# Local convolutions by head: 17 matmul passes with delayed column blocks and shifted copies, in place of 23

## The chip, the core and the metric

The program runs on one core of one Trainium2 chip. Its engines are TensorE (PE, matmuls), VectorE (DVE), ScalarE (ACT), GpSimd (POOL) and SyncE (SP, which only issues transfers). Each runs its own instruction stream and waits on semaphores. The metric is the device time of one execution in microseconds.

## The reference

The input is 16 sequences of 256 tokens with 128 features, all float32. Three blocks follow each other, each with a layer norm and a residual: a mixture of 8 experts (top 2), attention, and the same mixture again. The change is in the attention, in `multiscale_conv`, which acts on the values `v` of 4 heads with 32 channels each:

```python
def multiscale_conv(v, ms_w3, ms_w15, ms_w31, kernel_mix_w, channel_mixer_w):
    b, l, h, d = v.shape
    x = jnp.swapaxes(v.reshape(b, l, h * d), 1, 2)
    outs = [dwconv_causal(x, w) for w in (ms_w3, ms_w15, ms_w31)]
    y = jnp.concatenate(outs, axis=1)
    y = y.reshape(b, h, 3 * d, l).transpose(0, 3, 1, 2)
    y = y @ kernel_mix_w
    y = (y.reshape(b, l, h * d) @ channel_mixer_w).reshape(b, l, h, d)
    return y
```

Three causal convolutions of 3, 15 and 31 taps give 3 x 128 channels. They are laid one behind the other and cut anew into 4 heads of 96 rows. So head 0 reads the kernel of 3 taps alone, head 1 the rest of it and some of the 15 taps, head 2 the rest of the 15 taps and the first 32 channels of the 31 taps, and head 3 the other 96 channels of the 31 taps alone. Each head's 96 rows are mixed to 32 (`kernel_mix_w`), and the 128 results are mixed again (`channel_mixer_w`). Beside it the attention computes a delta rule in chunks of 32 tokens and a small network (gelu, softmax) that weighs convolution, delta rule and `v`; a normalisation and an output projection end it.

## The kernel before

The program is `route`, `experts` ("e1"), `attention`, `experts` ("e2"). In e1 GpSimd folds the convolutions' taps and `kernel_mix_w` into one 128x128 matrix for each lag, `full`, split into a high and a low part for PE (`lag_hi`, `lag_lo`).

**The passes.** A convolution at a lag is a matmul of the lag's matrix with the values shifted by that many tokens. A half `q` (of 8) covers 4 sequences and 128 tokens: one pass is 128x128 by 128x512, and each lag takes three (`vhi` by `lag_hi`, `vlo` by `lag_hi`, `vhi` by `lag_lo`). `scales(q, at, count)` (L1066) issues passes number `at` and onward. The far lags 15 to 30 fill only half of the output columns, so a pass takes two of them, the second in the other column half, to be delayed by one token when it is copied out: 8 orders in bank 0. The near lags 0 to 14 take 15 orders in bank 1. That is 23 orders, 69 passes a half.

**Behind them.** ACT copies the sums from PSUM: `keep_far` (three copies, two of which place the delayed half) and `keep_near` (one copy). `channels(q)` (L1214) multiplies both by `channel_mixer_w`, 8 instructions, and `keep_scales` copies the result.

**The stages.** The sequences are worked in 4 groups of 4. Stage g, from -1 to 3, runs the delta rule of group g while it projects and convolves group a = g+1 (`stage`, L1316). It has 16 slots: each of the 8 steps is a `read` (L1168), a slot, an `update` (L1188), a slot. A slot holds large passes: the keys and queries of group a (`keys`), then `scales(2g+1)` by the numbers in `SCALES_AT` (L1412; `SCALES_ALONE` in the last stage), then its values. After the slots comes a tail: for the halves of group g the hidden layer (`hide`), `logits`, `turn_means`, `turn_mixture` and `output`, with pieces of `scales(2a)` between them (`filler`), and then `channels(2a)`, `turn(g+2)` and the solving of the next group's chunks.

**What sets the order.** It is written out by hand for each engine, and each executes strictly in that order. In ACT's stage `route_power` (an exponential for the routing of the group before, L1952) comes before `silu_queries(a, 1)` (L1857). The far and near sums use the same two banks as the projections, so the first pass into a bank waits until its last content has been copied: `silued` for the queries, `zkept` for the sums. In the tail ACT's order is an exponential (`power`, L1925), gelu (L1920), `keep_far` (L1895 to L1897), square (L1929), exponential, root (L1933), `keep_mixture` (L1938), square, root, `keep_near` (L1902).

## Time and profile before

| | us |
|---|---|
| median of 3 runs | 1018.54 |
| lowest, highest | 1016.92, 1025.63 |
| profiled execution, its own time | 1015.78 |
| its span in the profile | 1014.0 |
| mean granted clock of PE, share of full speed | 0.938 |

The profiled execution is the shortest of the four numbers, so durations read from it belong to 1015.78 and not to the median. The attention takes roughly the stretch from 320 to 730 us of the span; what lies before and after it is routing and experts. Busy times of PE are modelled at the end of an instruction: passes that are shown with 0.40 us start 0.24 us apart.

### The profile page before, as it was taken

The numbers are of one execution on the slowest core, as the hardware profiler recorded it, in microseconds if no ns is written. First come the engines' busy times: TensorE is split into PE (matmuls) and PEld (weight loads), VectorE is DVE, ScalarE is ACT, GpSimd is POOL, SyncE is SP. The second block draws the span as 40 slices with busy tenths as digits, with TensorE's granted clock in tenths as the row PEclk, the third lists the DMA queues.
The fourth block names the chain that finished last, engine by engine and source line by source line (L and its number), as shares of the span: only waits on it lengthen the run. The fifth ranks groups of instructions, "written<-read, shape, count | busy, mean of one in ns | idle before, by whom it ended". The sixth has DMA issues, their size and how long they took to land. (4 is left out here: it accounts for less than half of the span.)

```text
span 1014.0 us, 27996 instructions
## 1 busy us (share of the span) xinstructions
PE 878.8 (87%) x11972; PEld 768.5 (76%) x11972; DVE 569.9 (56%) x1663; ACT 338.9 (33%) x648; POOL 448.7 (44%) x550
## 2 busy tenths in 40 slices
PE   7739998999858889997999899979873999999980
PEld 5629998999846667776777777867762899999980
DVE  6806556555366953575566635562462455555545
ACT  2214443444214121342325331521241444444420
POOL 2757897254533002850058036814603234444442
PEclk9859999999959979999999999998997999999995
DMA  8833543442140000000100000001100433433326
GB/s 287 325 112 112 161 140 98 134 127 78 38 109 22 1 6 22 2 1 3 35 4 1 8 29 14 2 7 33 47 7 28 136 107 115 129 120 128 121 80 171
DMA packets 66550, 78.56 MB, mean 77 GB/s; under 512 B 8752, under 2 KB 52704, under 8 KB 65402
## 3 DMA queue, kind: packets, MB, share of 16 engines
q1 hardware_dynamic: 57466, 60.03, 19.3%
q0 software_dynamic: 8960, 16.74, 5.1%
q8 instruction: 94, 1.54, 0.6%
q14 instruction: 30, 0.25, 0.1%
HBM read 47.92 MB, written 30.52 MB: 77 GB/s over the span
## 5 line engine op out<-in xcount | busy, mean ns | idle before, releaser
L763 DVE TENSOR_TENSOR e_hid<-e_sg,e_pu 128x320 f32<-128x320 f32 x256 | 124.6, 487 | 165.8 <-ACT e_sg L699 162.2
L256 POOL DMA_INDIRECT queue<-xn,slot x128 | 127.5, 996 | 182.8 <-PE a_pc L1188 59.8
L267 POOL DMA_INDIRECT token<-e_rows,e_token x120 | 121.2, 1010 | 153.9 <-DVE e_rows L729 111.0
L699 ACT ACTIVATE e_sg<-e_pg 128x320 f32<-128x320 f32 x256 | 112.2, 438 | 207.9 <-PE e_pg L654 207.7
L652 PE MATMUL e_pg<-e_xlo,e_whi 128*128 128x320 f32 x256 | 96.1, 375 | 6.4 <-DVE e_xlo L718 3.3
L625 PE MATMUL e_po<-expert,e_hid 128*128 128x128 f32 x640 | 84.2, 275 | 0.0
L1082 PE MATMUL a_pz<-a_vhi,lag_hi 128*128 128x512 f32 x184 | 79.3, 431 | 2.5 <-DVE a_vlo L1480 2.5
L625 PEld LDWEIGHTS e_po<-expert,e_hid 128*128 128x128 f32 x640 | 80.3, 191 | 0.1
L654 PE MATMUL e_pu<-e_xhi,e_whi 128*128 128x320 f32 x256 | 79.5, 311 | 0.0
L653 PE MATMUL e_pu<-e_xhi,e_wlo 128*128 128x320 f32 x256 | 79.5, 311 | 0.0
L652 PE MATMUL e_pu<-e_xlo,e_whi 128*128 128x320 f32 x256 | 79.4, 310 | 0.0
L653 PE MATMUL e_pg<-e_xhi,e_wlo 128*128 128x320 f32 x256 | 79.3, 310 | 0.0
L654 PE MATMUL e_pg<-e_xhi,e_whi 128*128 128x320 f32 x256 | 79.2, 309 | 0.0
L1082 PE MATMUL a_pz<-a_vlo,lag_hi 128*128 128x512 f32 x184 | 78.1, 425 | 0.0
L1082 PE MATMUL a_pz<-a_vhi,lag_lo 128*128 128x512 f32 x184 | 77.0, 418 | 0.0
L625 PE MATMUL e_po<-e_expert,e_hid 128*128 128x128 f32 x560 | 73.7, 275 | 0.0
L625 PEld LDWEIGHTS e_po<-e_expert,e_hid 128*128 128x128 f32 x560 | 70.5, 191 | 0.0
L262 POOL DMA_INDIRECT expert<-rows,slot x24 | 22.7, 947 | 98.8 <-DVEq L1451 75.6
L840 POOL TENSOR_TENSOR a_prod<-a_inv,a_nmat 128x31 f32<-128x31 f32 (+15 forms) x93 | 48.3, 519 | 38.0 <-DVE a_nmat L1532 31.0
L842 POOL TENSOR_TENSOR a_inv<-a_inv,a_prod 128x31 f32<-128x31 f32 (+15 forms) x93 | 58.1, 625 | 7.3
L652 PEld LDWEIGHTS e_pg<-e_xlo,e_whi 128*128 128x128 f32 x256 | 49.0, 192 | 8.4 <-issue 6.7
L653 PEld LDWEIGHTS e_pg<-e_xhi,e_wlo 128*128 128x128 f32 x256 | 49.2, 192 | 0.0
(303 smaller groups left out, 1902.8 us busy)
## 6 DMA issues: line engine op xcount, KB each, us to landing
e_xs<-queue SPq DMA_DIRECT2D x32, 322.5 KB, 3.5
expert<-wexp_in SPq DMA_DIRECT2D x14, 512.0 KB, 5.2
e_expert<-wexp_in SPq DMA_DIRECT2D x14, 512.0 KB, 5.4
queue<-r_zero SPq DMA_DIRECT2D x4, 1290.0 KB, 10.2
token<-r_zero SPq DMA_DIRECT2D x4, 1024.0 KB
expert<-wexp_in SPq DMA_DIRECT2D x14, 256.0 KB, 2.9
e_expert<-wexp_in SPq DMA_DIRECT2D x14, 256.0 KB, 2.7
xn<-token SPq DMA_DIRECT2D x7, 512.0 KB, 7.6
```

The costliest lines, as they stand in the source:

```text
L256: pool.indirect_dma_start(io.queue[c], bass.IndirectOffsetOnAxis(ap=k.slot[:, j, c:c + 1], axis=0), k.xn[:, j, :], None, bounds_check=SLOT ...
L262: pool.indirect_dma_start(dst, None, io.rows, bass.IndirectOffsetOnAxis(ap=slot, axis=0)).then_inc(got, 16)
L267: pool.indirect_dma_start(io.token[c], bass.IndirectOffsetOnAxis(ap=token, axis=0), src, None, bounds_check=NTOK - 1, oob_is_err=False).th ...
L625: mm = pe.matmul(po[:, s // 4, (s % 4) * P:(s % 4) * P + P], hid[par][:, f, s * P:s * P + P], w[par][:, 2, f * P:f * P + P], start=(f == 0 ...
L652: pe.matmul(out, whi[par][:, i, fs], xlo[par][:, cols], start=True, stop=False)
L653: pe.matmul(out, wlo[par][:, i, fs], xhi[par][:, cols], start=False, stop=False)
L654: pe.matmul(out, whi[par][:, i, fs], xhi[par][:, cols], start=False, stop=True).then_inc(gued, 1)
L699: act.activation(sg[n % 2][:], pg[n % 2][:, 0:HALF], ACT.Silu).then_inc(silued, 1)
L763: dve.tensor_tensor(hid[q % 2][:, f, c * HALF:c * HALF + HALF], sg[n % 2][:], pu[n % 2][:, 0:HALF], ALU.mult).then_inc(hidden, 1)
L840: link(eng.tensor_tensor(part, bc(inv[:, j:j + 1, 0:j + 1], shape), bc(factor, shape), ALU.mult))
L842: link(eng.tensor_tensor(rest, rest, part, ALU.add))
L1082: mm = pe.matmul(pz[:, bank, :].rearrange("p (s l) -> p s l", s=SEQS), w[:, j, :], x[:, :, start:start + P], start=first, stop=last)
```

## The change

The orders are packed by head. Order 0 ("apart") holds four lags of column blocks that need nothing more: head 0's three lags and head 3's lag 15. Each block is copied out with its own delay (0, 1, 2 and 15 tokens). Head 0 then needs no further pass, so its 32 columns in the 15 near orders carry head 3's lags 16 to 30, to be delayed by 16 tokens. Head 2's part of the 31 taps covers only 32 channels, and its lags 15 to 30 go into a single order ("stacked", order 11): SP copies those 32 channels four times below each other, shifted by 0, 1, 2 and 3 tokens (`shi`, `slo`), and the four column blocks are delayed by 0, 4, 8 and 12. That makes 17 orders, 51 passes a half. The column blocks that belong to the same head are summed in `channels`, whose weights (`channel_rows`) repeat the head's rows: three matmuls for a chunk in place of two. The blocks are placed by ACT, 32 partitions at a time: 7 copies for apart, 7 for stacked, 3 for near (`keep_part`). The counts in slots and fillers are smaller, and `load_expert` for e2 moves behind the copies of three groups.

```diff
@@ -47,7 +47,9 @@
 PAD = TAPS - 1
 LAGS = 31
 NEAR = 15
-FAR = (LAGS - NEAR) // 2
+ROWS = P // DH
+SPILL = 16
+PASSES = 2 + NEAR
 GRP = 8
 YB = NT
 SEQS = GRP * P // SEQ
...
@@ -179,38 +182,42 @@
-    def fold_far(self, pool, k):
...
+    def fold_apart(self, pool, k):
+
         w31 = lambda lag: self.ms31[:, LAGS - 1 - lag:LAGS - lag]
+        head = lambda h: slice(h * DH, h * DH + DH)
+        for lag in range(3):
+            pool.tensor_scalar(self.full[:, 0, head(lag)], self.base[:, 0, head(0)], self.ms3[:, 2 - lag:3 - lag], None,
+                               ALU.mult)
+        pool.tensor_scalar(self.full[:, 0, head(3)], self.base[:, 2, head(3)], w31(NEAR), None, ALU.mult)
+        for i in range(ROWS):
+            pool.tensor_scalar(self.full[:, 1, head(i)], self.mixs[:], self.ms31s[:, i:i + 1], None, ALU.mult)
+        for n in range(NEAR):
+            pool.tensor_scalar(self.full[:, 2 + n, head(3)], self.base[:, 2, head(3)], w31(n + SPILL), None, ALU.mult)
...
@@ -854,7 +861,9 @@
     UNITS, TURNS, TERMS = 6, 8, 3
     QUARTERS, QN = 4, NCH // 4
     KEYS, VALUES = 4 * TERMS * TAPS + 2 * TERMS, 2 * TERMS * TAPS
-    FARS, SCALES = TERMS * FAR, TERMS * (FAR + NEAR)
+    SCALES = TERMS * PASSES
+    STACKED_AT = 11
+    Z_APART, Z_STACKED, Z_NEAR = 0, 1, 2
     strip = lambda i: slice(i * CHUNK, i * CHUNK + CHUNK)
     with ExitStack() as ctx:
         m = Memory(nc, ctx)
...
@@ -945,10 +955,21 @@
+            for a in range(NGRP):
+                if a == NGRP - 1:
+                    sp.wait_ge(loaded[1], 16 * (NGRP - 1))
+                    sp.wait_ge(combined, NGRP)
+                    load_expert(sp, io, k.w, 0, loaded[1])
+                for half in range(HALVES):
+                    behind(sp, zdone, 6 * a + 3 * half - 1)
+                    for done, part, stack in ((vhigh, vhi, shi), (vlow, vlo, slo)):
+                        sp.wait_ge(done, 2 * a + 2)
+                        for r in range(ROWS):
+                            at = LAGS - 1 - NEAR - r + half * P
+                            sp.dma_start(stack[r * DH:r * DH + DH, :, :].bitcast(F32),
+                                         part[0:DH, :, at:at + P].bitcast(F32)).then_inc(shifted, 16)
+            sp.wait_ge(loaded[1], 16 * NGRP)
+            sp.wait_ge(shifted, 16 * 2 * ROWS * HALVES * NGRP)
 
         @block.gpsimd
         def _(pool):
...
@@ -1066,21 +1087,30 @@
             def scales(q, at, count):
                 a, half = divmod(q, 2)
                 for i in range(at, min(at + count, SCALES)):
-                    j, term = divmod(i, TERMS)
-                    lag = NEAR + 2 * j if j < FAR else j - FAR
-                    bank = 0 if j < FAR else 1
-                    first, last = i in (0, FARS), i in (FARS - 1, SCALES - 1)
-                    if first and half and a + 1 < NGRP:
+                    order, term = divmod(i, TERMS)
+                    kind = {0: Z_APART, STACKED_AT: Z_STACKED}.get(order, Z_NEAR)
+                    lag = order - 1 - (order > STACKED_AT) if kind == Z_NEAR else 0
+                    bank = 1 if kind == Z_NEAR else 0
+                    first = i == 0 or i == TERMS or i == TERMS * STACKED_AT
+                    last = i == TERMS - 1 or i == TERMS * STACKED_AT + TERMS - 1 or i == SCALES - 1
+                    if first and kind == Z_STACKED:
+                        pe.wait_ge(zkept, 3 * q + 1)
+                        pe.wait_ge(shifted, 16 * 2 * ROWS * (q + 1))
+                    elif first and half and a + 1 < NGRP:
                         pe.wait_ge(silued, UNITS * (a + 1) + 3 + bank)
                     elif first and half:
-                        pe.wait_ge(zkept, 4 * a + 1 + bank)
+                        pe.wait_ge(zkept, 6 * a + 2 + bank)
                     elif first:
                         pe.wait_ge(silued, UNITS * a + 5 + bank)
                         pe.wait_ge(vlow, 2 * a + 2)
-                    x, w = ((vhi, k.lag_hi), (vlo, k.lag_hi), (vhi, k.lag_lo))[term]
-                    start = LAGS - 1 - lag + half * P
-                    mm = pe.matmul(pz[:, bank, :].rearrange("p (s l) -> p s l", s=SEQS), w[:, j, :],
-                                   x[:, :, start:start + P], start=first, stop=last)
+                    if kind == Z_STACKED:
+                        x, w = ((shi, k.lag_hi), (slo, k.lag_hi), (shi, k.lag_lo))[term]
+                        start = 0
+                    else:
+                        x, w = ((vhi, k.lag_hi), (vlo, k.lag_hi), (vhi, k.lag_lo))[term]
+                        start = LAGS - 1 - lag + half * P
+                    mm = pe.matmul(pz[:, bank, :].rearrange("p (s l) -> p s l", s=SEQS), w[:, kind + lag, :],
+                                   x[:, :, start:start + P], start=term == 0 and (kind < Z_NEAR or lag == 0), stop=last)
                     if last:
                         mm.then_inc(zdone, 1)
                 return min(at + count, SCALES)
...
@@ -1213,16 +1243,16 @@
...
                 for i in range(HCH):
-                    pe.matmul(pp[:, 1, i * P:i * P + P], chunks(znear[:], i), k.chan[:], start=True, stop=False)
-                    mm = pe.matmul(pp[:, 1, i * P:i * P + P], chunks(zfar[:], half * HCH + i), k.chan_far[:],
-                                   start=False, stop=True)
+                    for n, part in enumerate(z):
+                        mm = pe.matmul(pp[:, 1, i * P:i * P + P], chunks(part[:], half * HCH + i), k.chan[:, n, :],
+                                       start=(n == 0), stop=(n == 2))
                 mm.then_inc(chaned, 1)
 
             def turn_means(q):
...
@@ -1375,20 +1405,20 @@
...
-                part = filler(9)
+                part = filler(6)
                 idle(g, 9)
                 if here:
                     hide(2 * g + 1, 0)
                     hide(2 * g + 1, 1)
-                part = filler(12)
+                part = filler(9)
                 idle(g, 4)
                 if here:
                     logits(2 * g + 1)
-                part = filler(12)
+                part = filler(9)
                 idle(g, 24)
                 if here:
                     turn_mixture(2 * g)
-                part = filler(9)
+                part = filler(6)
                 idle(g, 3)
                 if here:
                     output(2 * g)
...
@@ -1409,11 +1439,11 @@
                     solve_keys(a, 0)
 
             KEYS_AT = (12, 8, 12, 8, 14)
-            SCALES_AT = (0, 0, 0, 0, 0, 8, 7, 7, 7, 7, 8, 8, 8, 9)
-            SCALES_ALONE = (5, 4, 6, 4, 6, 6, 6, 6, 6, 6, 6, 6, 2)
+            SCALES_AT = (0, 0, 0, 0, 0, 6, 6, 5, 5, 5, 6, 6, 6, 6)
...
@@ -1885,22 +1915,35 @@
                 act.activation(u[:, half * HCH:half * HCH + HCH, :, :].rearrange("p n s d -> p (n s d)"), pp[:, 2, :],
                                ACT.Copy).then_inc(ukept, 1)
 
-            def keep_far(q):
-                half = q % 2
-                act.wait_ge(zdone, 2 * q + 1)
+            def keep_part(q, kind, first, end, delay):
+                head, at = slice(first * DH, end * DH), q % 2 * HCH
+                raw = pz[head, kind // 2, :].rearrange("p (s n c) -> p n s c", s=SEQS, n=HCH)
+                last = act.activation(z[kind][head, at:at + HCH, :, delay:], raw[:, :, :, 0:CHUNK - delay], ACT.Copy)
+                if delay:
+                    over = HCH - q % 2
+                    last = act.activation(z[kind][head, at + 1:at + over + 1, :, 0:delay],
+                                          raw[:, 0:over, :, CHUNK - delay:], ACT.Copy)
+                return last
+
+            def keep_apart(q):
+                act.wait_ge(zdone, 3 * q + 1)
                 behind(act, chaned, q)
-                far = D // 2
-                z = pz[:, 0, :].rearrange("p (s n c) -> p n s c", s=SEQS, n=HCH)
-                at = half * HCH
-                act.activation(zfar[0:far, at:at + HCH, :, 1:], z[0:far, :, :, 0:CHUNK - 1], ACT.Copy)
-                act.activation(zfar[0:far, at + 1:at + HCH + 1, :, 0:1], z[0:far, :, :, CHUNK - 1:], ACT.Copy)
-                act.activation(zfar[far:D, at:at + HCH, :, :], z[far:D], ACT.Copy).then_inc(zkept, 1)
+                for h, delay in enumerate((0, 1, 2, NEAR)):
+                    last = keep_part(q, Z_APART, h, h + 1, delay)
+                last.then_inc(zkept, 1)
+
+            def keep_stacked(q):
+                act.wait_ge(zdone, 3 * q + 2)
+                behind(act, chaned, q)
+                for i in range(ROWS):
+                    last = keep_part(q, Z_STACKED, i, i + 1, ROWS * i)
+                last.then_inc(zkept, 1)
 
             def keep_near(q):
-                act.wait_ge(zdone, 2 * q + 2)
+                act.wait_ge(zdone, 3 * q + 3)
                 behind(act, chaned, q)
-                act.activation(znear[:], pz[:, 1, :].rearrange("p (s n c) -> p n s c", s=SEQS, n=HCH),
-                               ACT.Copy).then_inc(zkept, 1)
+                keep_part(q, Z_NEAR, ROWS - 1, ROWS, SPILL)
+                keep_part(q, Z_NEAR, 0, ROWS - 1, 0).then_inc(zkept, 1)
 
             def keep_scales(q):
                 act.wait_ge(chaned, q + 1)
...
@@ -1979,10 +2022,12 @@
                     root_keys(a)
                 if later:
                     root_rows(g + 2)
+                if here:
+                    keep_apart(2 * g + 1)
                 if ahead and here:
                     measure(a)
                 if here:
-                    keep_far(2 * g + 1)
+                    keep_stacked(2 * g + 1)
                     keep_values(g, 0)
                     keep_values(g, 1)
                     keep_near(2 * g + 1)
...
@@ -2000,11 +2045,11 @@
                     gelu(2 * g, 1)
                     keep_means(2 * g + 1)
                     power(2 * g)
+                if ahead:
+                    keep_apart(2 * a)
                 if here:
                     gelu(2 * g + 1, 0)
                     gelu(2 * g + 1, 1)
-                if ahead:
-                    keep_far(2 * a)
                 if here:
                     square(2 * g)
                     power(2 * g + 1)
...
@@ -2013,6 +2058,7 @@
                     square(2 * g + 1)
                     root_mix(2 * g + 1)
                 if ahead:
+                    keep_stacked(2 * a)
                     keep_near(2 * a)
                     keep_scales(2 * a)
                 if later:
...
```

**ScalarE, in the tail of stage 1**, between the exponential of the second half and the square of the first (`a_lg` are the logits, `a_hdn` the hidden layer, `a_pz` the sums in PSUM). Before:

```order
L1925 ACTIVATE a_lg<-a_lg 128x48 [waits a_lowered]
L1920 ACT_TABLE_LOAD [waits a_scored,a_gated]
L1920 ACTIVATE a_hdn<-a_pp,b 128x512 [waits a_hidden]
L1920 ACTIVATE a_hdn<-a_pp,b 128x512 [waits a_scored,a_gated,a_hidden]
L1895 ACTIVATE a_zfar<-a_pz 64x16x31 [waits a_chaned,a_zdone]
L1896 ACTIVATE a_zfar<-a_pz 64x16
L1897 ACTIVATE a_zfar<-a_pz 64x512
L1929 ACTIVATE a_direct<-a_delta 128x512 [waits a_mixed]
```

and changed:

```order
L1968 ACTIVATE a_lg<-a_lg 128x48 [waits a_lowered]
L1921 ACTIVATE a_z<-a_pz 32x512 [waits a_chaned,a_zdone]
L1921 ACTIVATE a_z<-a_pz 32x16x31
L1924 ACTIVATE a_z<-a_pz 32x16
L1921 ACTIVATE a_z<-a_pz 32x16x30
L1924 ACTIVATE a_z<-a_pz 32x16x2
L1921 ACTIVATE a_z<-a_pz 32x16x17
L1924 ACTIVATE a_z<-a_pz 32x16x15
L1963 ACT_TABLE_LOAD [waits a_scored,a_gated]
L1963 ACTIVATE a_hdn<-a_pp,b 128x512 [waits a_hidden]
L1963 ACTIVATE a_hdn<-a_pp,b 128x512 [waits a_scored,a_gated,a_hidden]
L1972 ACTIVATE a_direct<-a_delta 128x512 [waits a_mixed]
```

The copies of bank 0 stand ahead of gelu now, and there are seven in place of three.

**ScalarE, at the end of the same tail**, from the last square. Before:

```order
L1929 ACTIVATE a_direct<-a_delta 128x512 [waits a_mixed]
L1933 ACTIVATE a_ors<-a_oss,eps 128x16 [waits a_summed]
L1902 ACTIVATE a_znear<-a_pz 128x512 [waits a_chaned,a_zdone]
L1908 ACTIVATE a_ms<-a_pp 128x512 [waits a_mixed,a_chaned]
L1938 ACTIVATE a_oT<-a_pc 128x4x4x32 [waits a_done,a_oturned]
```

and changed:

```order
L1972 ACTIVATE a_direct<-a_delta 128x512 [waits a_mixed]
L1976 ACTIVATE a_ors<-a_oss,eps 128x16 [waits a_summed]
L1921 ACTIVATE a_z<-a_pz 32x512 [waits a_chaned,a_zdone]
L1921 ACTIVATE a_z<-a_pz 32x16x28
L1924 ACTIVATE a_z<-a_pz 32x16x4
L1921 ACTIVATE a_z<-a_pz 32x16x24
L1924 ACTIVATE a_z<-a_pz 32x16x8
L1921 ACTIVATE a_z<-a_pz 32x16x20
L1924 ACTIVATE a_z<-a_pz 32x16x12
L1921 ACTIVATE a_z<-a_pz 32x16x16 [waits a_chaned,a_zdone]
L1924 ACTIVATE a_z<-a_pz 32x16x16
L1921 ACTIVATE a_z<-a_pz 96x512
```

Behind the root, where one copy stood, there are ten: seven of the stacked order and three of the near orders.

**TensorE, in slot 5 of stage 1**, from the delta rule's output matmuls of the update to the next read (`a_sq` are the squares of keys and queries). Before:

```order
L1194 MATMUL a_po<-a_u,a_loc 32x32 x16
L1082 MATMUL a_pz<-a_vhi,lag_hi 128x512 [waits a_silued]
L1082 MATMUL a_pz<-a_vlo,lag_hi 128x512
L1082 MATMUL a_pz<-a_vhi,lag_lo 128x512
L1082 MATMUL a_pz<-a_vhi,lag_hi 128x512
L1093 MATMUL a_pp<-const,a_sq 64x4 [waits a_mskept,a_squared]
L1093 MATMUL a_pp<-const,a_sq 64x4 x7
L1082 MATMUL a_pz<-a_vlo,lag_hi 128x512
L1082 MATMUL a_pz<-a_vhi,lag_lo 128x512
L1082 MATMUL a_pz<-a_vhi,lag_hi 128x512
L1082 MATMUL a_pz<-a_vlo,lag_hi 128x512
L1168 MATMUL a_pc<-a_state,a_wT 32x32 [waits a_stated]
```

and changed:

```order
L1224 MATMUL a_po<-a_u,a_loc 32x32 x16
L1112 MATMUL a_pz<-a_vhi,lag_hi 128x512 [waits a_silued]
L1112 MATMUL a_pz<-a_vlo,lag_hi 128x512
L1112 MATMUL a_pz<-a_vhi,lag_lo 128x512
L1123 MATMUL a_pp<-const,a_sq 64x4 [waits a_mskept,a_squared]
L1123 MATMUL a_pp<-const,a_sq 64x4 x7
L1112 MATMUL a_pz<-a_vhi,lag_hi 128x512 [waits a_silued]
L1112 MATMUL a_pz<-a_vlo,lag_hi 128x512
L1112 MATMUL a_pz<-a_vhi,lag_lo 128x512
L1198 MATMUL a_pc<-a_state,a_wT 32x32 [waits a_stated]
```

The slot has six passes in place of eight, and its fourth, the first of the near orders, carries a wait for `silued` that stood at the 25th pass of the half before.

## Rows read from the trace of the kernel before

**Rows 1.** The page's first part: busy time, share of the span, instructions.
```profile
PE 878.8 (87%) x11972; PEld 768.5 (76%) x11972; DVE 569.9 (56%) x1663; ACT 338.9 (33%) x648; POOL 448.7 (44%) x550
```
**Rows 2.** Windows: stretch, length, busy time by engine, clock, DMA share, GB/s.
```profile
core 0: us, PE busy (x) PEld busy (x) DVE busy (x) ACT busy (x) POOL busy (x), PEclk, DMA share, GB/s
362.00:428.00 66.00, 64.18 (x1662) 48.28 (x1654) 31.72 (x85) 15.11 (x25) 27.26 (x44) 0.98 0.04 11
536.00:567.00 31.00, 29.00 (x155) 23.36 (x154) 23.51 (x41) 15.58 (x23) 16.99 (x29) 1.00 0.00 1
680.00:729.00 49.00, 42.87 (x1312) 32.65 (x1299) 17.89 (x87) 7.00 (x13) 25.30 (x26) 0.91 0.12 37
467.00:471.00 4.00, 4.00 (x31) 2.67 (x33) 2.38 (x17) 1.53 (x2) 0.00 (x0) 0.57 0.02 4
```
**Rows 3.** Timeline of PE, tail of stage 0: start, duration, what, idle before it.
```profile
452.94 0.39 PE L1082 MATMUL a_pz<-a_vlo,lag_hi 128*128 128x512 f32 x1
...
456.01 0.40 PE L1082 MATMUL a_pz<-a_vhi,lag_lo 128*128 128x512 f32 x1
```
**Rows 4.** Timeline of PE, end of stage -1.
```profile
356.91 0.32 PE L1139 MATMUL a_pp<-a_vh,a_low 32*32 32x32 f32 x6 [5.25 <-DVE a_low L1540]
```
**Rows 5.** Timeline of PE, tail of stage 1.
```profile
551.23 1.85 PE L1260 MATMUL a_pp<-w,a_hdn 128*128 128x12 f32 x16
...
557.30 0.66 PE L1270 MATMUL a_pp<-const,a_delta 128*128 128x128 f32 x4 [1.30 <-DVE a_delta L1631]
...
565.24 0.49 PE L1223 MATMUL a_pp<-chan,a_znear 128*128 128x128 f32 x2 [0.69 <-ACT a_znear L1902]
...
567.13 1.04 PE L1021 MATMUL a_pz<-const,xn 128*128 128x128 f32 x8
```
**Rows 6.** Timeline of ACT and PE, slot 5, and of ACT, tail, of stage 1.
```profile
496.37 0.21 ACT L1952 ACTIVATE a_ratio<-a_gap 128x8 f32<-128x8 f32 x1 [4.39 <-DVE a_gap L1647]
...
497.89 0.60 ACT L1857 ACTIVATE a_kq<-a_pz 128x512 f32<-128x512 f32 x1
497.90 0.45 PE L1168 MATMUL a_pc<-a_state,a_wT 32*32 32x32 f32 x32
...
546.46 0.24 ACT L1925 ACTIVATE a_lg<-a_lg 128x48 f32<-128x48 f32 x1
...
549.29 0.58 ACT L1895 ACTIVATE a_zfar<-a_pz 64x496 f32<-64x496 f32 x1
549.77 0.18 ACT L1896 ACTIVATE a_zfar<-a_pz 64x16 f32<-64x16 f32 x1
549.96 0.59 ACT L1897 ACTIVATE a_zfar<-a_pz 64x512 f32<-64x512 f32 x1
552.27 0.63 ACT L1929 ACTIVATE a_direct<-a_delta 128x512 f32<-128x512 f32 x1 [1.71 <-DVE a_delta L1621]
...
562.69 0.31 ACT L1933 ACTIVATE a_ors<-a_oss,eps 128x16 f32<-128x16 f32 x1 [0.75 <-DVE a_oss L1625]
564.59 0.60 ACT L1902 ACTIVATE a_znear<-a_pz 128x512 f32<-128x512 f32 x1 [1.59 <-PE a_pz L1082]
```
**Rows 7.** Timeline of DVE, slots 9 to 13 of stage 1.
```profile
512.66 0.62 DVE L1518 TENSOR_TENSOR a_low<-a_pp,a_bvk 128x256 f32<-128x256 f32 x1 [2.17 <-PE a_pp L1121]
...
518.67 4.78 DVE L1466 TENSOR_SCALAR xn<-x,a_mv,a_rstd 128x128 f32<-128x128 f32 x8
523.37 0.28 DVE L1554 TENSOR_TENSOR a_u<-a_u,a_pc 128x128 f32<-128x128 f32 x1
```
**Rows 8.** Timeline of PE, start of stage 1.
```profile
466.13 0.25 PE L1154 MATMUL a_po<-a_nmat,a_kn 32*32 32x32 f32 x5 [1.95 <-issue]
...
467.68 0.63 PE L1027 MATMUL a_pz<-a_xhi,tap_lo 128*128 128x512 f32 x1
...
470.24 0.63 PE L1027 MATMUL a_pz<-a_xhi,tap_lo 128*128 128x512 f32 x1
```
**Rows 9.** The page's sixth part: transfers by line, KB each, us to landing.
```profile
xn<-token SPq DMA_DIRECT2D x7, 512.0 KB, 7.6
```

71 lines of the change are left out of this document (38 added, 33 removed).

## Prediction, made before the changed kernel was run

> **What bounds the kernel now.** I read the page's totals first, then the windows of the attention part, then the timeline of TensorE (PE) and ScalarE (ACT) where the changed work stands. The totals make PE the candidate: busy 87% of the span [rows 1]. The windows say where that is true. In the slots of stage 0 PE is busy 64.18 of 66.00 us at a granted clock of 0.98 [rows 2]; in the tail of stage 1 it is busy 29.00 of 31.00 us [rows 2], but its large passes there are filler, placed between steps of a chain that runs through ACT and VectorE (DVE). So a removed pass is worth its time only where PE would otherwise have been the last to arrive.
>
> A pass costs its pitch, not its busy time of 0.40 us, whose end is modelled. Fourteen passes start from 452.94 to 456.01 [rows 3], 13 steps: **0.236 us**.
>
> **What is removed and added on PE.** Each of the 8 halves loses 6 lags of 3 terms, 18 passes, 4.25 us; over 8 halves 34.0 us. `channels` grows from 8 to 12 instructions: 8 take 565.24 to 567.13, 1.89 us [rows 5], so 4 more are **+0.9 us** per half, 7.2 us in all. Were PE alone the bound, the balance would be -26.8 us. The following goes through the places one by one.
>
> **Stage -1.** PE waits 5.25 us for DVE before `solve_values` [rows 4]; the 18 passes removed ahead of it lengthen that wait. Saving 0. The added 0.9 us of `channels` stands ahead of the same wait and is covered too.
>
> **Slots of stages 0 to 3** (`scales(2g+1)`: 18 passes less, 4.25, less 0.9 for `channels`: at most -3.35 us each).
> - Stage 0: PE-bound throughout [rows 2], but DVE's eight normalising instructions take 4.78 us in a row ahead of a subtraction (the same in stage 1, at 518.67 [rows 7]), which I let take 0.4 back: **-3.0**.
> - Stage 1: a new wait. The first near pass comes fourth now, not 25th, so it stands in slot 5; its bank is released by `silu_queries(a,1)`, which ACT starts at 497.89 and ends at 498.49, behind `route_power` (an exponential at 496.37, then a table load) [rows 6]. Before, that slot ended with the read at 497.90 [rows 6]. Now three near passes follow 498.49: the read comes at about 499.3, +1.4, with the slot's own two saved passes in it. Queued behind the waiting pass is the whole recurrence. Slots 6 to the middle of 9 save 6 passes, -1.4. From there DVE is bound: it works from 512.66 to 523.45 almost without a gap, ends with the normalising and only then does the subtraction for which `update(1, 6)` waits [rows 7]; of the passes saved there I count 0.5. Slot 13 saves 3, -0.7; `channels` +0.9. Sum -0.3, rounded for the small delays of the longer ACT copies to **0.0**.
> - Stage 2: the same wait in slot 5 (+1.4) but no normalising; slots 6 to 13 save 16 passes, -3.8, `channels` +0.9: **-1.5**.
> - Stage 3: four passes per slot are left where there were mostly six; the window has PE busy 42.87 of 49.00 us [rows 2], so nearly all of the 3.35 counts: **-3.2**.
> Sum of the slots **-7.7**. `keep_stacked(2g+1)` stands ahead of `keep_values` on ACT and delays it by some 2 us; PE needs that copy's bank a slot later, over 3 us, so it costs nothing; without that distance it would cost up to 2 us per stage.
>
> **Tails of stages 0 to 2**, by stage 1's. The chain goes: ACT's exponential at 546.46, DVE's mixture, ACT's square at 552.27, and by way of sums, a root and a rescaling to `turn_mixture` at 557.30, before which PE already waited 1.30 us [rows 5, 6]. Nothing in it is a filler pass: removing 9 passes ahead of `turn_mixture` saves **0**, and its wait grows. `keep_apart(2a)` now stands right behind the exponential and delays gelu by its 2.5 us: gelu ended at 549.28, when `keep_far` started [rows 6], and ends at 551.8. PE, 0.7 us earlier than before and with 9 fillers rather than 12 behind `hide`, would be at `logits(2g+1)` at 549.8 instead of 551.23 [rows 5] and waits 2 us; logits end 0.6 us later than before, and ACT is free for the square at 552.27 [rows 6]. DVE takes those logits only after a sum behind the square, so the chain stands: 0.
>
> **The end of the tail** is where I expect the loss. Before, ACT did one copy of 0.60 us behind the second root (562.69 to 563.00), and it waited 1.59 us for PE's last pass; `channels` started at 565.24 [rows 5, 6]. Now `keep_stacked` (7 copies) and `keep_near` (3) both stand behind that root. No row shows copies of 32 partitions; the nearest are of 64: 496 elements occupy ACT 0.48 us (549.29 to 549.77), 16 elements 0.19 (to 549.96) [rows 6]. Between them, by elements (512, 448+64, 384+128, 320+192), `keep_stacked` takes 0.49 + 0.67 + 0.67 + 0.67 = 2.5 us, and `keep_near` 0.33 + 0.33 + 0.5 = 1.2. Bounds: 0.49 for every copy gives 3.4 and 1.5; a cost by elements alone (2.0 and 1.0) the other end. ACT, not PE, is last: 563.00 + 3.7 = 566.7, **+1.5** (bounds +0.8 to +2.7), and `channels` itself +0.9: +2.4 per tail. Behind it stand `turn(g+2)` and `solve_values`; PE goes straight on there [rows 5], so it is not given back. Three tails: **+7.2**.
>
> **The clock.** PE now idles some 4 us ahead of `channels` instead of 0.69 [rows 5]. After a wait of 1.95 us at 466.13 the passes from 467.68 to 470.24 stand 0.427 us apart, not 0.236, and the granted clock of that stretch is 0.57, the 1.2 GHz level for most of it [rows 2, 8]: seven passes, 1.3 us lost. I take one such stretch for each tail, 3.9, less one that stage 0 has already in this place (the one of rows 8): **+2.6**. Bounds: 0 (the idle shifts, it adds none) and twice that.
>
> **What costs nothing.** The 16 copies of 32 channels per group, issued by SP: no row has a copy within the on-chip memory; the nearest are 512 KB in 7.6 us [rows 9], each of these is 64 KB. The passes that read them are 33 passes behind the start of their half, over 8 us of passes alone and 15 us with what stands between them, and the buffers are free since the last half. If they came late, the stacked passes would wait with everything behind them (rival 3). SP also holds back the load of the next experts' weights behind the copies of groups 0 to 2; it is used only after the attention. GpSimd's folding of weights lies in the first experts part, beside PE work, and gets slightly shorter.
>
> **The sum.** -7.7 + 7.2 + 2.6 = **+2.1 us**. The profiled execution took 1015.78 (span 1014.0), so the changed one 1017.9. The median of the runs shown, 1018.54, lies 2.76 above the profiled one: **1020.7 us**. Its own range, from the bounds (copies -2.1/+3.6, clock -2.6/+2.6, slot waits -3/+3) and the scatter of the runs: 1012 to 1029.
>
> **Rivals.**
> 1. PE-bound everywhere. For it: 87% busy, windows of 93 to 97%. Against: PE's waits of 5.25 and 1.30 us stand just where passes are removed [rows 4, 5]. It would give -26.8: 991.7. Chance 0.07. The Trainium skill's page "Perfetto Trace Analysis", section "Identifying the Most-Contended Engine", says to optimise the engine with the highest occupancy first, and that TensorE's headroom is not judged by matmul busy time; its first half points to this rival, its second is why busy time is weak evidence here.
> 2. Slots give all, tails lose nothing. Copies of 32 partitions are as cheap as the lower bound and hidden, and the slot-5 wait is not there because `silu_queries` comes early when PE runs ahead. 4 x -3.35 = -13.4: 1005.1. For it: stage 0's window [rows 2]. Against: slot 5's rows [rows 6]. Chance 0.15.
> 3. Slower: the tail's end. From the point where the ten copies take over 4.5 us (or the stacked copies land late), PE idles over 5 us ahead of `channels`, and the whole of `turn`, `solve` and the first `keys` runs at the lower clock. Copies at the upper bound add 1.2 per tail; low-clock stretches three times those of rows 8 add 2.6 more: 3 x 3.8 = 11.4 over the forecast: 1032. For it: ACT's late place is certain from the order of the program. Against: ACT's interpolated prices. Chance 0.18.
>
> The forecast has 0.60. Within 1% of 1018.54 (1008.4 to 1028.7; about what a measurement of this kernel tells from no change) lies most of the forecast: 0.56 there, 0.02 on either side. Rival 2 lies below 1008.4, as does 1: faster 0.24; slower 0.20. The range that holds 8 in 10 leaves out rival 1 and the upper half of rival 3: **1003 to 1031**.
>
> **What would show it.** PE in stage 1's slot 5 idles 1.5 to 2 us before a near pass, released by ACT's `a_kq` copy (right), or not (rival 2). Each of the first three tails shows PE idle 3 to 5 us ahead of `channels`, released by ACT's last `a_z` copy; ACT's seven stacked copies sum to 2.2 to 2.8 us. `turn_mixture(2g)` stands as far behind the exponential as before (10.8 us). The granted clock in the slices behind the tails falls below 0.9. Wrong it would be if the idle time ahead of `channels` stays under 2 us, if the slots of stages 0 and 3 do not get 3 us shorter, or if a pass waits for SP's copies.

## The result and the profile after

| | before | changed |
|---|---|---|
| median of 20 runs, us | 1018.64 | 1023.42 |
| lowest, highest | 1012.49, 1025.63 | 1018.29, 1031.44 |
| profiled execution, its span | 1015.78, 1014.0 | 1022.46, 1020.4 |
| mean granted clock | 0.938 | 0.923 |

The ratio is 1.0057 (95% interval 1.0039 to 1.0076): 5 to 6 us slower, within 1%. The forecast was +2.1 us, 1020.7 for the median.

The first part of the page of the changed kernel, for [rows 1]:

```profile
PE 863.1 (85%) x11892; PEld 757.5 (74%) x11892; DVE 565.2 (55%) x1665; ACT 373.0 (37%) x752; POOL 444.3 (44%) x557
```

PE has 15.7 us less to do and the span is 6.4 us longer: PE's busy time was not what the end hung on. ACT has 34.1 us more.

Where time goes and comes back is read by subtracting the starts of the same instruction in both traces:

| first instruction of | before | changed | later by |
|---|---|---|---|
| `solve_values`, group 0 | 356.91 | 353.46 | -3.45 |
| `update`, step 0, stage 0 | 366.43 | 364.27 | -2.16 |
| `channels`, slot 15, stage 0 | 425.16 | 418.39 | -6.77 |
| `solve_values` behind tail 0 | 460.39 | 458.80 | -1.59 |
| `update`, step 0, stage 1 | 470.80 | 466.29 | -4.51 |
| `update`, step 2 (ahead of slot 5), stage 1 | 493.90 | 489.56 | -4.34 |
| `update`, step 3, stage 1 | 501.67 | 501.26 | -0.41 |
| `channels`, slot 15, stage 1 | 533.31 | 530.39 | -2.92 |
| `turn_mixture(2)` | 557.30 | 555.42 | -1.88 |
| `channels` at the end of tail 1 | 565.24 | 564.76 | -0.48 |
| `solve_values` behind tail 1 | 568.53 | 570.57 | +2.04 |
| `update`, step 0, stage 2 | 576.25 | 578.33 | +2.08 |
| `channels`, slot 15, stage 2 | 639.28 | 641.28 | +2.00 |
| `solve_values` behind tail 2 | 673.63 | 681.82 | +8.19 |
| `update`, step 0, stage 3 | 679.78 | 687.42 | +7.64 |
| `channels`, slot 15, stage 3 | 726.13 | 728.44 | +2.31 |
| `turn_mixture(7)` | 753.56 | 756.96 | +3.40 |
| span | 1014.0 | 1020.4 | +6.4 |

The attention of the kernel before starts at 296 us and reaches `turn_mixture(7)` at 754, so its stretch is wider than the 320 to 730 given above. Of the +6.4 us of the span, three parts can be told apart: -3.4 ahead of its first gate pass (303.06, not 306.50), +6.8 from there to `turn_mixture(7)`, and +3.0 behind that.

**Ahead of the attention.** The program differs there only in what GpSimd folds. The last folding instruction, which makes `lag_lo`, has 2176 columns for 2944 and takes 4.89 us for 6.80. In both kernels one VectorE instruction of the first experts part starts while it runs and ends only when it has ended. Before, that was one that PE needed:

```profile
164.62 6.80 POOL L220 TENSOR_TENSOR lag_lo<-full,lag_hi 128x2944 fp32r<-128x2944 f32 x1
166.64 5.33 DVE L710 TENSOR_TENSOR e_wlo<-expert,e_whi 128x512 fp32r<-128x512 f32 x1
172.51 0.39 PE L652 MATMUL e_pg<-e_xlo,e_whi 128*128 128x320 f32 x1 [2.91 <-DVE e_hid L763]
```

and changed, where PE has no wait behind it:

```profile
160.92 4.89 POOL L227 TENSOR_TENSOR lag_lo<-full,lag_hi 128x2176 fp32r<-128x2176 f32 x1
162.88 2.95 DVE L746 TENSOR_SCALAR e_token<-e_xs 128x5 uint32<-128x5 f32 x1
```

The same VectorE instruction (`e_wlo`) takes 0.68 us when nothing holds it. The first gate pass starts at 303.1 to 304.6 in the changed kernel and in E2, E3, E4, E9, E10 and E12, which fold as it does, and at 309.2 in E1, which folds as before. In E11 it starts at 306.4 although it folds as the changed kernel: there VectorE's `e_token` is held for 4.81 us and PE waits 1.81. So the gain belongs to the change in most executions; no run separates it, and why VectorE is held isn't shown.

**Inside the attention.** Slots gain (from the first `update`, 4.6 us in stage 0 and 5.3 in stage 3), each tail loses 5 to 6, and stages 1 and 2 gain next to nothing in their slots, for the most part because of one wait in slot 5. E9, the same kernel once more, loses 10.2 us by the same cut in its profiled execution, which took 1027.72: its tails agree (+15.4 for +16.3 us) and its slots gain less (3.9 for 8.4). Single terms of the slots are thus good to some microseconds only.

**Behind it.** The 3.0 us are lost before the second experts part, at a granted clock of 0.69 in the window from 763 to 773 us, where the same stretch before (760 to 770) has 1.00. E2, E4 and E9 lose 2.5 to 3.5 us there as well, E3, E10, E11 and E12 0 to 1.0, so it is not a fixed price of the change.

Slot 5 of stage 1, PE and then ACT, timelines of the changed kernel (start, duration, what, idle before it):

```profile
490.25 0.51 PE L1112 MATMUL a_pz<-a_vhi,lag_hi 128*128 128x512 f32 x1
490.59 0.40 PE L1112 MATMUL a_pz<-a_vlo,lag_hi 128*128 128x512 f32 x1
490.83 0.40 PE L1112 MATMUL a_pz<-a_vhi,lag_lo 128*128 128x512 f32 x1
491.15 1.09 PE L1123 MATMUL a_pp<-const,a_sq 128*64 128x4 f32 x16
494.21 0.79 PE L1112 MATMUL a_pz<-a_vhi,lag_hi 128*128 128x512 f32 x1 [1.96 <-ACT a_kq L1887]
494.80 0.63 PE L1112 MATMUL a_pz<-a_vlo,lag_hi 128*128 128x512 f32 x1
495.23 0.63 PE L1112 MATMUL a_pz<-a_vhi,lag_lo 128*128 128x512 f32 x1
495.78 0.65 PE L1198 MATMUL a_pc<-a_state,a_wT 32*32 32x32 f32 x32
```
```profile
492.04 0.21 ACT L1995 ACTIVATE a_ratio<-a_gap 128x8 f32<-128x8 f32 x1 [4.37 <-DVE a_gap L1677]
492.26 1.28 ACT L1887 ACT_TABLE_LOAD   x1
493.56 0.60 ACT L1887 ACTIVATE a_kq<-a_pz 128x512 f32<-128x512 f32 x1
```

The first near pass waits 1.96 us for a copy that itself stood behind an exponential [rows 6]. What the wait leaves behind costs time as well: the passes behind it start 0.43 us apart instead of 0.24, and the window says why. Windows of the changed kernel: the slots of stage 0, tail 1, the slots of stage 3, the stretch behind that wait, and `channels` in tail 1:

```profile
358.00:422.00 64.00, 62.63 (x1718) 47.03 (x1714) 31.05 (x85) 19.39 (x38) 26.37 (x43) 0.95 0.05 12
534.00:570.00 36.00, 29.99 (x154) 24.39 (x153) 23.76 (x41) 20.34 (x38) 17.78 (x30) 0.91 0.19 52
682.00:731.00 49.00, 41.64 (x1563) 32.28 (x1553) 19.93 (x92) 12.49 (x28) 24.50 (x25) 0.95 0.12 37
494.00:500.00 6.00, 5.79 (x134) 4.24 (x134) 1.04 (x5) 4.95 (x12) 0.00 (x0) 0.50 0.01 3
565.00:569.00 4.00, 4.00 (x23) 4.00 (x23) 0.35 (x1) 0.00 (x0) 0.00 (x0) 0.57 0.02 4
```

The tail of stage 1 had a granted clock of 1.00 [rows 2] and has 0.91; the six microseconds behind slot 5's wait run at 0.50, the 1.2 GHz level.

The middle of tail 1, PE, of the changed kernel, from the logits to `turn_mixture(2)`:

```profile
549.78 1.95 PE L1290 MATMUL a_pp<-w,a_hdn 128*128 128x12 f32 x16 [1.55 <-ACT a_hdn L1963]
...
553.32 0.63 PE L1112 MATMUL a_pz<-a_vlo,lag_hi 128*128 128x512 f32 x1
553.74 0.63 PE L1112 MATMUL a_pz<-a_vhi,lag_lo 128*128 128x512 f32 x1
...
555.42 0.66 PE L1300 MATMUL a_pp<-const,a_delta 128*128 128x128 f32 x4
```

PE waits for gelu, ahead of which the seven apart copies now stand, and the nine fillers behind the logits run 0.43 us apart. So PE reaches `turn_mixture` with no wait in tails 0 and 1, and with 1.67 us of it in tail 2, where these fillers run 0.24 apart.

The end of tail 1, ACT and then PE, of the changed kernel; the first row is the root behind which one copy stood [rows 6]:

```profile
560.81 0.31 ACT L1976 ACTIVATE a_ors<-a_oss,eps 128x16 f32<-128x16 f32 x1 [0.75 <-DVE a_oss L1655]
561.02 1.12 ACT L1921 ACTIVATE a_z<-a_pz 32x512 f32<-32x512 f32 x2
562.05 0.20 ACT L1924 ACTIVATE a_z<-a_pz 32x64 f32<-32x64 f32 x1
562.26 0.48 ACT L1921 ACTIVATE a_z<-a_pz 32x384 f32<-32x384 f32 x1
...
563.47 0.36 ACT L1921 ACTIVATE a_z<-a_pz 32x256 f32<-32x256 f32 x1
563.73 0.36 ACT L1924 ACTIVATE a_z<-a_pz 32x256 f32<-32x256 f32 x1
564.11 0.59 ACT L1921 ACTIVATE a_z<-a_pz 96x512 f32<-96x512 f32 x1
```
```profile
564.76 4.57 PE L1254 MATMUL a_pp<-chan,a_z 128*128 128x128 f32 x24 [4.23 <-ACT a_z L1921]
569.17 1.04 PE L1042 MATMUL a_pz<-const,xn 128*128 128x128 f32 x8
```

The seven stacked copies take 561.02 to 563.47, 2.45 us; the near ones until 564.70, 1.23. PE idles 4.23 us where it idled 0.69, and then runs `channels` in 4.41 us (564.76 to 569.17) where 8 instructions took 1.89 [rows 5]. In stage -1 the same 24 matmuls take 2.78 us to the next start, behind 1.34 us of idle time, so 1.6 us of it is clock. In tails 0 and 2 PE idles 3.26 and 4.23 us and `channels` takes 4.15 and 5.28.

### The profile page after: what moved, and what is told of

Its sections match the earlier page's. It is cut to its first block and busy times, and to the rows that moved or that the text cites. A ratio compares the mean times of both kernels' runs of the same rounds, so it can differ in the third digit from the quotient of the medians.

```text
span 1020.4 us, 28035 instructions
## 1 busy us (share of the span) xinstructions
PE 863.1 (85%) x11892; PEld 757.5 (74%) x11892; DVE 565.2 (55%) x1665; ACT 373.0 (37%) x752; POOL 444.3 (44%) x557
## 5 line engine op out<-in xcount | busy, mean ns | idle before, releaser
L847 POOL TENSOR_TENSOR a_prod<-a_inv,a_nmat 128x31 f32<-128x31 f32 (+15 forms) x93 | 50.3, 540 | 41.1 <-DVE a_nmat L1562 34.1
L1112 PE MATMUL a_pz<-a_vhi,lag_hi 128*128 128x512 f32 x128 | 59.9, 468 | 6.5 <-ACT a_kq L1887 3.9
L849 POOL TENSOR_TENSOR a_inv<-a_inv,a_prod 128x31 f32<-128x31 f32 (+15 forms) x93 | 55.8, 599 | 7.3
L1112 PE MATMUL a_pz<-a_vlo,lag_hi 128*128 128x512 f32 x128 | 55.0, 430 | 0.0
L1112 PE MATMUL a_pz<-a_vhi,lag_lo 128*128 128x512 f32 x128 | 54.6, 426 | 0.0
L1921 ACT ACTIVATE a_z<-a_pz 32x512 f32<-32x512 f32 (+3 forms) x80 | 40.9, 512 | 28.7 <-PE a_pz L1112 28.0
```

Source lines behind the costliest of these rows:

```text
L847: link(eng.tensor_tensor(part, bc(inv[:, j:j + 1, 0:j + 1], shape), bc(factor, shape), ALU.mult))
L849: link(eng.tensor_tensor(rest, rest, part, ALU.add))
L1112: mm = pe.matmul(pz[:, bank, :].rearrange("p (s l) -> p s l", s=SEQS), w[:, kind + lag, :], x[:, :, start:start + P], start=term == 0 and ...
L1921: last = act.activation(z[kind][head, at:at + HCH, :, delay:], raw[:, :, :, 0:CHUNK - delay], ACT.Copy)
```

## The experiments

Twelve more runs were made, in three rounds. Ratios are to the kernel before, run in the same round: its median is 1017.31 us beside E1 to E4, 1057.56 beside E5 to E8, and 1019.90 beside E9 to E12, so only ratios compare between rounds. The changed kernel stands at 1.0057 and, run again as E9, at 1.0043: 1.005. It did not run in the rounds of E1 to E8, and where a run is compared with it there, this 1.005 is carried over, with an interval of about 0.002 of its own.

**E1, lags dropped: what the missing passes are worth.** The kernel before, less six far orders, with the counts of the changed kernel in slots and fillers:

```diff
-    FARS, SCALES = TERMS * FAR, TERMS * (FAR + NEAR)
+    FARS, SCALES = TERMS * 2, TERMS * (2 + NEAR)
```

> The kernel before, with the last six of its eight far orders left out (18 of 69 passes per half, so the output lacks those lags) and the slot and filler counts of the changed kernel. All else is as before: four copies on ScalarE, two matmuls per chunk in channels, no transfers by SP. It prices the removal of passes alone. My theory: only the slots pay (13 us over four stages, less than 4 x 4.25 because VectorE takes some back), and in each of three tails channels starts 1.5 us earlier, when the root is done: about -17 us, 1002. Rival (TensorE is the bound everywhere): 8 x 4.25 = -34, 985. If it lies near 1018, even the slots pay nothing.

Measured 1005.6, ratio 0.9895 (0.9863 to 0.9927): -10.7 us, of 34 that the passes take. The rival of a PE-bound kernel is out, and my own -17 was too high. New idle time shows why; PE's waits in tails 0 and 1:

```profile
448.31 0.66 PE L1270 MATMUL a_pp<-const,a_delta 128*128 128x128 f32 x4 [3.08 <-DVE a_delta L1631]
454.54 0.49 PE L1223 MATMUL a_pp<-chan,a_znear 128*128 128x128 f32 x2 [1.16 <-ACT a_znear L1902]
...
551.14 0.66 PE L1270 MATMUL a_pp<-const,a_delta 128*128 128x128 f32 x4 [3.12 <-DVE a_delta L1631]
```

`turn_mixture` waited 1.30 [rows 5] and waits 3.1: the fillers ahead of it were free in the kernel before.

**E2, one copy of each kind: what ACT's pieces cost.**

```diff
-                for i in range(ROWS):
-                    last = keep_part(q, Z_STACKED, i, i + 1, ROWS * i)
+                last = keep_part(q, Z_STACKED, 0, ROWS, 0)
```
(and the same for the other two kinds)

> The changed kernel with one copy of 128x512 for each of the three kinds of sums instead of 7, 7 and 3 (the delays are left out, so the convolution is wrong). Passes, waits, transfers and matmuls stay. My theory: behind the root of each tail stand 1.2 us of copies instead of 3.7, so channels starts 2.5 us earlier in three tails, and the low-clock stretch behind the idle time shrinks by 0.5 to 1 each: -9 to -10 us from 1023.4, about 1014. Rival (the loss sits in the third matmul of channels, in slot 5 or in SP's transfers): within 3 us of 1023.

Measured 1008.29, ratio 0.9924 (0.9894 to 0.9955): -1.3% of the changed kernel's time, some -13 us, more than the 9 to 10 expected. ACT at the end of tail 1:

```profile
553.43 0.31 ACT L1973 ACTIVATE a_ors<-a_oss,eps 128x16 f32<-128x16 f32 x1 [0.75 <-DVE a_oss L1655]
553.64 1.06 ACT L1921 ACTIVATE a_z<-a_pz 128x512 f32<-128x512 f32 x2
```

Two copies of 128 partitions take 1.06 us for the ten pieces' 3.68. PE then idles 1.64 us ahead of `channels` in tails 0 and 1 and 0.69 in tail 2, and `channels` takes 2.78 us in all three. So E2 takes away the copies' length and the lower clock behind it together: the pieces with what they cause are enough to turn the sign, for without them the kernel lies below the one before.

**E3, three passes in slot 5.**

```diff
-            SCALES_AT = (0, 0, 0, 0, 0, 6, 6, 5, 5, 5, 6, 6, 6, 6)
+            SCALES_AT = (0, 0, 0, 0, 0, 3, 6, 6, 6, 6, 6, 6, 6, 6)
```

> The changed kernel with 3 passes in slot 5 (the apart order alone) and 6 in every later slot (0,0,0,0,0,3,6,6,6,6,6,6,6,6), so that the first near pass stands in slot 6, behind a read. My theory: the idle time of 1.96 us before it in stages 1 and 2 goes, and with it the stretch at the lower clock behind it (six passes 0.43 apart, a gram of 1.93 for 1.10): 2 to 2.5 us per stage net of what VectorE keeps, -4 to -5, about 1019. Rival (it only moves into slot 6, or VectorE's chain takes it all): within 1.5 us of 1023.4.

Measured 1019.48, ratio 1.0029 (1.0002 to 1.0056), some 2 us below the changed kernel and not clear of noise: the intervals overlap. The wait got shorter and did not go; the first near pass in slot 6 of stages 1 and 2:

```profile
494.68 0.50 PE L1112 MATMUL a_pz<-a_vhi,lag_hi 128*128 128x512 f32 x1 [1.07 <-ACT a_kq L1887]
...
604.85 0.76 PE L1112 MATMUL a_pz<-a_vhi,lag_hi 128*128 128x512 f32 x1 [1.02 <-ACT a_kq L1887]
```

Here, moving work away from a late event only halved the wait and moved it; the event has to come earlier.

**E4, the stacked copies ahead of the second square.**

```diff
                     keep_mixture(2 * g)
+                if ahead:
+                    keep_stacked(2 * a)
+                if here:
                     square(2 * g + 1)
                     root_mix(2 * g + 1)
                 if ahead:
-                    keep_stacked(2 * a)
                     keep_near(2 * a)
```

> The changed kernel with keep_stacked(2a) on ScalarE right behind keep_mixture(2g), ahead of the second square, where the trace has 2.71 us of idle time, instead of behind the last root. My theory: the seven copies (2.45 us) fit there, only keep_near (1.23) stays behind the root, and channels starts 2.2 us earlier in each of three tails, with a smaller stretch at the lower clock: -7 to -10, about 1015. Rival (the copies do not fit and delay square and root by as much): within 2 us of 1023.4; then the tail's end is bound by ScalarE's whole load.

Measured 1013.51, ratio 0.9965 (0.994 to 0.999): -9 us from the changed kernel. ACT in tail 1:

```profile
555.78 0.60 ACT L1981 ACTIVATE a_oT<-a_pp 128x512 f32<-128x512 f32 x1 [1.76 <-PE a_pp L1300]
556.28 1.12 ACT L1921 ACTIVATE a_z<-a_pz 32x512 f32<-32x512 f32 x2
...
558.51 0.31 ACT L1924 ACTIVATE a_z<-a_pz 32x192 f32<-32x192 f32 x1
559.09 0.63 ACT L1972 ACTIVATE a_direct<-a_delta 128x512 f32<-128x512 f32 x1 [0.27 <-DVE a_delta L1651]
```

They end before the square could start: it still waits 0.27 us for DVE. PE's wait ahead of `channels` falls from 4.23 to 1.91 us, and `channels` takes 2.78 us.

**E5, the exponential behind the queries.**

```diff
-                if past:
-                    route_power(r)
                 if ahead:
                     silu_queries(a, 1)
+                if past:
+                    route_power(r)
+                if ahead:
                     root_keys(a)
```

> The changed kernel with ScalarE's route_power moved behind silu_queries(a,1), so that the bank of the near passes is freed before slot 5 and not behind an exponential that waits for VectorE. My theory: the idle time of 1.96 us in slot 5 of stages 1 and 2 and the low-clock stretch behind it go: -4 to -6 from 1023.4, about 1018.5. In the trace no near pass of stages 1 and 2 waits for a_kq. Rival (VectorE's chain in slots 9 to 13 binds the stage anyway): -2 or less.

Ratio 1.0021 (0.9998 to 1.0045), 0.3% below the changed kernel, about -3 us and so less than the 4 to 6 expected; the intervals touch. No near pass of stages 1 and 2 waits for `a_kq` any more. Around slot 5 the changed kernel lost 3.9 us in stage 1 and 2.7 in stage 2 (+2.23 at 601.41, +4.88 at 611.83), so 6.6 in all. In E5's trace the stretch between the updates of steps 2 and 3 takes 7.06 and 9.03 us in stages 1 and 2, in E6 of the same round, which keeps the wait, 11.49 and 11.24. The wait is thus removed and a part of what that saves is taken back behind; which link takes it was not separated.

**E6, dummy matmuls in the idle time: is it the clock?**

```diff
                 part = filler(SCALES)
+                if ahead and here:
+                    keep_clock(pe, k, pp[:, 1, :], 30)
```

> The changed kernel with 30 dummy matmuls (bf16, 128x256, about 3.4 us, into the PSUM bank that channels writes next) behind the last filler pass in the tails of stages 0 to 2, where TensorE idles 3.3 to 4.2 us. They remove idle time and no work. My theory: channels starts when it did (ScalarE's copies decide), but runs at the high level, 2.9 us and not 4.3 to 4.6, and what follows too: -1.5 per tail, -4 to -5 from 1023.4, about 1019. Rival (the slow channels is not due to the idle time ahead of it): 1023 or, with dummies in the way, later.

Ratio 1.0001 (0.9975 to 1.0027): -0.5% from the changed kernel, 5 us, by work that computes nothing; the interval just touches that of E9. PE at the end of tail 0, and the window with `channels` in it:

```profile
470.50 3.45 PE L479 MATMUL a_pp<-const 128*128 128x256 bf16 x30
473.82 2.94 PE L1254 MATMUL a_pp<-chan,a_z 128*128 128x128 f32 x24
476.61 1.04 PE L1042 MATMUL a_pz<-const,xn 128*128 128x128 f32 x8
```
```profile
474.00:478.00 4.00, 4.00 (x36) 3.84 (x36) 0.52 (x2) 1.19 (x3) 0.00 (x0) 1.00 0.02 4
```

`channels` takes 2.79 us to the next start, not 4.15, at a clock of 1.00. From the start of `channels` to `solve_values` the three tails take 4.2, 4.2 and 3.3 us, in the changed kernel 5.6, 5.8 and 6.0: 5.6 us less, with the same instructions in between, which agrees with the ratio.

**E7, E4's and E5's moves together.**

> The changed kernel with both moves on ScalarE: keep_stacked(2a) ahead of the second square, and route_power behind silu_queries(a,1). The places are apart, so the gains should add: -9 and -5 from 1023.4, about 1009, which is 9 us faster than the kernel before. Rival (one wait covers the other): not below 1013.

Ratio 0.9893 (0.9857 to 0.9929): -1.6%, against -0.9% and -0.3% alone. They add, within the intervals.

**E8, dummies on top (14).**

> As the run before, with 14 dummy matmuls (1.6 us) in the idle time of about 1.9 us that is left ahead of channels in three tails. My theory: channels of stage 0's tail, and what follows in the others, keeps the high level: -1 to -3 from the run before, about 1007. Rival: the idle time left is too short to matter, no difference beyond 1 us.

Ratio 0.988 (0.984 to 0.9919). Not to be told from E7, although the dummies did what they were for: `channels` takes 2.78 us in all three tails, in E7 4.08, 2.78 and 4.41. A gain of 2.9 us lies within the noise of two times six executions, so E8 neither confirms nor refutes E6.

**E9, the changed kernel again.**

> The changed kernel itself once more, unaltered, as the reference for the three runs beside it. Ratio to the kernel before as measured first: 1.0057 (1.004 to 1.008). Rival: if it lies at 1.000 or at 1.012 here, chips differ by as much as the effects, and differences between the runs of different chips below 0.6% mean nothing.

1025.32, ratio 1.0043 (1.0024 to 1.0062).

**E10, no transfers.**

```diff
-                            sp.dma_start(stack[r * DH:r * DH + DH, :, :].bitcast(F32),
-                                         part[0:DH, :, at:at + P].bitcast(F32)).then_inc(shifted, 16)
+                            pass
```
(with the waits on `shifted` gone and the four copies set to zero once)

> The changed kernel without SP's 64 transfers of 32 channels (the four shifted copies are zeros throughout, so the stacked order adds nothing). Passes, ScalarE's copies and channels stay. My theory: the copies land long before the passes that read them: no difference from the run of the changed kernel beside it beyond 2 us. Rival (they hold back TensorE or other transfers): 4 us or more faster.

1033.58, ratio 1.012 (1.0085 to 1.0155): *slower* than E9 by 8 us, which neither theory has. Its six runs lie from 1025.14 to 1039.23; the profiled one is the fastest (span 1023.3 against E9's 1025.6), and in its trace `channels` of tail 0 starts at 452.95, E9's at 453.04. So the trace shows no cost of the transfers and none of leaving them out. The five slower executions have a mean granted clock of 0.905 to 0.914, the profiled one 0.922 and E9's twelve 0.912 to 0.925: they were slower at a lower clock. What lowered it no profile shows, and it stays open. That the transfers are hidden rests on the changed kernel's trace: no row of a stacked pass waits for them, and a transfer lands in 2.1 us:

```profile
a_shi<-a_vhi SPq DMA_DIRECT2D x32, 64.0 KB, 2.1
```

**E11, two matmuls in `channels`.**

```diff
-                    for n, part in enumerate(z):
+                    for n, part in ((0, z[0]), (2, z[2])):
```

> The changed kernel with two matmuls per chunk in channels, the stacked sums left out of the product (they are still computed and copied). My theory: 0.9 us per half at the high level, 1.5 where channels runs at the low one (three tails and the last stage), nothing in stage -1: -7 to -9 from the run of the changed kernel beside it. Rival (the chain behind absorbs it): -3 or less.

1021.75, ratio 1.0015 (0.9993 to 1.0038); the medians lie 3.6 us below E9 in the same round. That is nearer to the rival's 3 than to the 7 to 9 of the theory: the third matmul costs about half of eight times its 0.9 us, and the scatter leaves room for 1.5 to 5.5 us.

**E12, a third move: `keep_near(2a)` between the second square and its root.**

```diff
                 if here:
                     square(2 * g + 1)
+                if ahead:
+                    keep_near(2 * a)
+                if here:
                     root_mix(2 * g + 1)
```

> Both moves on ScalarE (route_power behind silu_queries, keep_stacked ahead of the second square) and a third: keep_near(2a) between the second square and the second root, where ScalarE waits 0.75 us for VectorE. The root is needed only behind channels. My theory: channels starts 0.7 us earlier again in three tails: ratio to the kernel before 0.987, against 0.9893 without the third move. Rival (near passes end too late for it, and the delayed root holds back turn_mixture(2g+1)): 0.989 or more.

1003.33, ratio **0.9833** (0.9806 to 0.986): 17 us faster than the kernel before and 22 faster than the changed one beside it (E9), with all of its computation. It is the median of five executions. ACT and PE in tail 1:

```profile
553.99 0.38 ACT L1921 ACTIVATE a_z<-a_pz 32x256 f32<-32x256 f32 x1 [2.23 <-PE a_pz L1112]
554.27 0.36 ACT L1924 ACTIVATE a_z<-a_pz 32x256 f32<-32x256 f32 x1
554.65 0.59 ACT L1921 ACTIVATE a_z<-a_pz 96x512 f32<-96x512 f32 x1
555.14 0.29 ACT L1976 ACTIVATE a_ors<-a_oss,eps 128x16 f32<-128x16 f32 x1
```
```profile
555.29 2.94 PE L1254 MATMUL a_pp<-chan,a_z 128*128 128x128 f32 x24 [1.34 <-ACT a_z L1921]
```

ACT now waits for PE (2.23 us) ahead of its last copies; PE's idle time is 1.34 us and `channels` takes 2.78 us to the next start, in all three tails.

## Why the prediction was right, point by point

- **The sum: right, in part by luck.** The forecast's +2.1 us all lie inside the attention, where the profiled execution loses 6.8. Two amounts that it put at nothing add to that: -3.4 ahead of the attention ("What costs nothing" has the folding slightly shorter) and +3.0 behind it. Inside, by the table and in the forecast's terms: entry of stage 0 +1.3 (0 forecast), slots -8.4 (-11.3), tails with their clock +16.3 (+12.5), starts of stages 1 to 3 -3.4 (0), last tail +1.1 (+0.9).
- **Direction and mechanism: right.** Seen in the trace and in E1, E2, E4. A removed filler pass was worth nothing ahead of `turn_mixture` (E1's 3.1 us of wait), and the copies behind the root were dear (E2, E4). From the exponential to `turn_mixture` tail 1 took 10.84 us (546.46 to 557.30) and takes 10.99 (544.43 to 555.42), as forecast.
- **The wait ahead of `turn_mixture`: wrong.** It was to grow from 1.30 us and is gone in tails 0 and 1. The forecast had PE's wait at the logits (2 us; measured 1.5) and not the lower clock behind it, which takes up the time that the removed fillers leave. In tail 1 that cost nothing.
- **ACT's copies: right.** 2.45 and 1.23 us against 2.5 and 1.2; `channels` in tail 1 starts 1.4 us later against the chain, forecast 1.5.
- **Stage -1: right in the saving (0).** PE's wait grew from 5.25 [rows 4] to 8.86 us and it starts as much earlier (3.45) as the attention is entered. From there to the first `update` 1.3 us are lost that the forecast did not have; in E9 they are not lost, so they belong to this execution.
- **Slot 5: the wait right (1.96 us), the term wrong.** Its clock was left out. Between the updates of steps 2 and 3 stage 1 loses 3.9 us (-4.34 to -0.41), the forecast had the read 1.4 later. From the first `update` to slot 15 stage 1 loses 1.6 where (without `channels`) -0.9 was forecast, stage 2 gains 0.1 of 2.4.
- **Tails: too small.** From `channels` in slot 15 to `solve_values`: 5.2, 5.0 and 6.2 us, together 16.3. The forecast by the same cut is 3 x (0.9 + 2.4) and 2.6 for the clock, 12.5. The mis-sized term is the clock: 1.3 us per tail was taken from seven passes of one row group; `channels` alone loses 1.4, 1.6 and 2.5 to it, 5.5 us, and E6 gives back 5 to 6.
- **What gave back.** The low stretch that stage 1 had at its start [rows 8] is gone: 2.9 us come back between `solve_values` and `update`, where 1.3 was counted. Stage 3's slots gain 5.3 us (4.1 forecast), a part of it clock as well: its window stands at 0.95 and stood at 0.91 [rows 2]. These and the 3.4 us ahead of the attention offset the mis-sized terms, which is why the sum lies closer than its parts.
- **The signs.** PE idles 3.26, 4.23 and 4.23 us ahead of `channels` (3 to 5 forecast), the slots of stages 0 and 3 get more than 3 us shorter, and no pass waits for SP's copies. The granted clock falls below 0.9 in the page's slices of tails 0 and 2 and not in that of tail 1.
- **Rivals.** PE-bound: excluded by E1. The rule to optimise the engine with the highest occupancy first (the Trainium skill, "Perfetto Trace Analysis", section "Identifying the Most-Contended Engine") pointed there; here the engine at 87% got 34 us less to do in E1 for 10.7 us of time. Rival 2's cheap slots and tails: both fail, the slots by slot 5's wait; the order of ACT that it would need is E7's. Rival 3's conditions are not met (its copies of over 4.5 us are 3.68, its idle time of over 5 us is 4.23), and only its lower clock behind `channels` shows in part: +5 to 6 us, not +13.

## What to carry to other kernels

Before passes are taken off the busiest engine, mark for each of them what ends the wait behind it: in E1, 34 us of work were worth 11. When the result of a matmul is to be placed in pieces, each piece is paid on the copying engine, and the pieces belong where that engine waits for somebody, not behind the last link of its chain: the seven stacked copies cost 9 us more behind the root than ahead of the square (E4). A bank that is filled earlier needs its last reader moved earlier as well.
